# Group pipelines around the typed attention and the message pass of a four-layer graph network, with products made as rows and weights laid out ahead

## The chip, the cores and the metric

The kernel runs on one NeuronCore of one Trainium2 chip. The metric is the device time of one execution in microseconds (us). TensorE (PE) is clocked at one of two levels, 1.2 or 2.4 GHz; the profile gives the granted clock as a share of the full one. All arithmetic is in float32 unless bf16 is named.

## The reference

A graph of 3125 nodes with 128 features and 50000 edges, sorted by destination, goes through four residual layers. Each has the form `x = x + layer(relu(layernorm(x)))`.

```
x = x + gine(h)        3 rounds: relu(x[src] + ea64 @ We) summed per dst, two products, norm
x = x + rel_att(h)     for each of 5 edge types r: softmax over the edges of one dst of
                       leaky(Q_r[dst].a_q + K_r[src].a_k), sum of V_r[src] * attn; then elu
x = x + typed_att(h)   below
x = x + message(h)     below

typed_att:  Q, K, V = h @ block-diagonal W_Q, W_K, W_V of the node's type (3 types, 8 heads of 16)
            kt = K[src] @ W_edge[edge type]         (5 types)
            score = (Q[dst] * kt).sum(-1) / sqrt(16) * mu[head, edge type]
            w = softmax(score) over the edges of one dst; agg = sum of V[src] * w
            h1 = layernorm(h + agg @ W_out + b_out) * g1 + b1
            y  = layernorm(h1 + gelu(h1 @ W1 + b1) @ W2 + b2) * g2 + b2'
message:    m = relu([h[src], h[dst], ea32] @ W1.T + b1) @ W2.T + b2;  agg = sum of m per dst
            y = layernorm(h + relu(agg @ Wu.T + bu)) * gamma + beta
```

## The kernel before, in words

**Tiling.** The nodes are padded to 25 blocks of 128 rows (`NBLK`), and a node array is a tile of 128 x 3200. The edges lie in 416 tiles of 128 slots, so that no tile straddles a block; four tiles make one of 104 batches. "Groups" are 7 runs of up to four blocks (the last has one), 512 columns, one PSUM bank each. Products of whole arrays (`product`, L1709) run over 8 groups of 400 columns.

**Edge loops.** Each layer has one or two loops over the 104 batches. The five engines each have a program of their own; `run(engine, stages)` walks the batches and calls each stage with its lag, so that engines are several batches apart and wait for each other's semaphores. Every batch of a gathering loop takes four indirect DMAs of 128 rows on GpSimd (POOL): from `table_rel` (L714, first relation attention: value rows per node and edge type), `table_keys_values` (L723, typed attention: rows of 256 values, one per node and edge type), and `table_msg` (L696, message pass). Sums per destination are products with one-hot tiles, added to an array in SBUF or, where a sum stays in PSUM over a whole loop, opened and closed by seven products of one zero row (128x512, L1940, L2031, L2058).

**Order of the work around the change.** Between loops the program goes through stages that are separated by `Join` barriers: `join.to("x")` makes an engine wait until all engines have arrived there. In order:

- `rel_vectors`: PE makes for every block the value rows of the 5 edge types (L1866 128x512, L1867 128x128), ACT evacuates them (L1527, L1528), SP writes them to `table_rel`. Then come the score lookups over the batches (`lookups`, L1879, L1880, with DVE `pick_k`, L1100), while POOL gathers ahead and the values go to DRAM; then softmax sums per segment; then the loop `att_lookups`/`att_sums`. Its sums lie in seven PSUM banks.
- `rel_out`: ELU and the norm over the whole 128 x 3200 array on DVE (`norm`, L745 to L770; per-block statistics by L748, then 3200-column operations).
- `tr_clear` to `tr_values`: masks of the three node types multiply the array into three copies (L739), 75 transposes (L1698) with ACT copies of 512 columns (L1436), keys with the typed weights (L1709, 24 of 400 columns), Q and V (L2017, 75 of 256 columns) with ACT copies and bf16 splits of Q into three parts on DVE (`split`), then keys by edge type (L2024, L2025), which DVE multiplies by `mu` while it evacuates (L739, 125 of 128x128), and SP writes keys and values to `table_keys_values`.
- `trA` and `trB`: two loops over the batches, the first for scores and maxima with the gathers, the second for the weighted sums; `tr_zero` between them.
- `tr_mean` to `tr_out`: division by the softmax sum, 25 transposes, the product with W_out in transposed form, transposes back, sum and norm, 25 transposes, four hidden products with Gelu on ACT, the product with W2, transposes back, sum, norm, sum with X, norm. SP loads the weights of each part when the stage begins.
- `mp_weights` to `mp_table`: transposes, products of the two node parts of W1, one evacuated by DVE as node terms (L739 128x512), the other transposed back into the table and written in one DMA of 1600 KB.
- `mp`: per batch DVE makes a one-hot (float32, L739 128x512), PE transposes it (L1951) and ACT copies it (L1584); PE adds for each tile the edge product (L2103) and the lookup of node terms (L2104); DVE adds the gathered rows, ACT takes the ReLU, PE sums (L1734), DVE accumulates.
- `mp_sumT` to `mp_out`: transposes of the sums and of the degrees, product with W2 plus a one-row product for the bias (L1709, b2row), product with Wu, transposes back, norm, last sum and the output in two DMAs.

## Time and profile before

| what | value |
| --- | --- |
| three runs | 5188.26, 5188.58, 5203.77 us (median 5188.58) |
| profiled execution, its own time | 5186.52 us |
| its span in the trace | 5184.8 us |
| mean granted clock | 0.747 |
| busy: PE, DVE, POOL, ACT | 3185.8 (61%), 2685.6 (52%), 2938.1 (57%), 782.1 (15%) us |
| DMA | 561.85 MB, mean 108 GB/s |

No engine is busy for more than 61% of the span, so the shares alone name no bound: stages with different limits follow each other. A line of the profile's list of groups names the source line, the engine, the operation, what it writes and reads, the shape and the count; behind the first bar come busy time and the mean of one in ns, behind the second the idle time of the engine just before these instructions and what ended most of it. A float32 product has two records in such lists.

### The profile page before, as it was taken

What the parts mean: (1) busy time and instruction counts of PE and PEld (TensorE: products, weight loads), DVE (VectorE), ACT (ScalarE), POOL (GpSimd) and SP (SyncE); (2) the same over time, 40 slices, a digit from 0 to 9 for tenths busy, and PEclk for the clock granted to TensorE, in tenths of its full rate; (3) what the DMA queues carried; (4) which work ended last, traced back from release to release, by engine and by line L of the source; (5) the groups of instructions that cost most, each with busy time, mean ns of one, the idle gap of its engine ahead of it and who ended that gap; (6) DMA issues with size and microseconds to landing.
All of it is one profiled execution on the core that took longest, in us unless ns stands there. A gap on an engine that the chain in (4) does not pass through costs nothing. (4 is left out here: it accounts for less than half of the span.)

```text
span 5184.8 us, 84388 instructions
## 1 busy us (share of the span) xinstructions
PE 3185.8 (61%) x20680; PEld 2748.7 (53%) x20681; DVE 2685.6 (52%) x7818; ACT 782.1 (15%) x1810; POOL 2938.1 (57%) x2911
## 2 busy tenths in 40 slices
PE   0000298885777677775554676657776886566665
PEld 0000188885666566664552465445655884356663
DVE  5100288875444444445679655356664664344443
ACT  1000022222111111112100243100000001222222
POOL 3767677774777477771677740067773000077772
PEclk9999989886555555556655798855555997799997
DMA  6333355553222322222872573466654441022222
GB/s 214 75 87 77 93 153 151 150 140 76 76 76 77 60 77 75 76 76 62 214 202 88 172 193 100 109 170 174 175 171 106 123 127 47 4 72 62 62 61 32
DMA packets 631530, 561.85 MB, mean 108 GB/s; under 512 B 236605, under 2 KB 523650, under 8 KB 631426
## 3 DMA queue, kind: packets, MB, share of 16 engines
q0 software_dynamic: 99328, 211.51, 17.4%
q1 hardware_dynamic: 392322, 233.28, 15.5%
q10 hardware_dynamic: 139776, 115.91, 7.9%
q8 instruction: 38, 0.62, 0.0%
q14 instruction: 66, 0.54, 0.0%
HBM read 408.99 MB, written 151.40 MB: 108 GB/s over the span
## 5 line engine op out<-in xcount | busy, mean ns | idle before, releaser
L696 POOL DMA_INDIRECT ring<-table_gine,idx x1248 | 1244.2, 997 | 496.8 <-issue 370.3
L696 POOL DMA_INDIRECT ring<-table_msg,idx x416 | 425.0, 1022 | 725.4 <-SPq L191 598.9
L739 DVE TENSOR_TENSOR mraw<-ps,ring 128x512 f32<-128x512 f32 x416 | 287.4, 691 | 827.0 <-DMA ring<-table_gine,idx 372.4
L723 POOL DMA_INDIRECT arena<-table_keys_values,idx x416 | 429.7, 1033 | 466.1 <-SPq L191 337.8
L1777 PE MATMUL ps<-oh,msg 128*128 128x128 f32 x1664 | 425.5, 436 | 307.5 <-DVE HA L739 211.7
L714 POOL DMA_INDIRECT HA<-table_rel,idx x416 | 444.5, 1068 | 253.8 <-DMA table_rel<-arena 127.3
L739 DVE TENSOR_TENSOR HA<-HA,ps 128x128 f32 (+1 forms) x1664 | 476.5, 286 | 166.9 <-DVE HA L739 146.2
L1777 PEld LDWEIGHTS ps<-oh,msg 128*128 128x128 f32 x1664 | 366.4, 324 | 366.1 <-DVE HA L739 337.1
L1744 PE MATMUL ps<-wt,ear 65*128 65x128 f32 x2496 | 521.1, 379 | 16.7 <-DMA ear<-edge_attr_T 16.7
L682 POOL DMA_INDIRECT slot_records<-arena,slotr x400 | 390.3, 976 | 214.6 <-issue 122.2
L1744 PEld LDWEIGHTS ps<-wt,ear 65*128 65x128 f32 x2496 | 494.1, 293 | 17.4 <-issue 16.9
L739 DVE TENSOR_TENSOR oh<-iota_n,dl 128x512 f32<-128x512 f32 x624 | 431.0, 691 | 40.9 <-DVE small L739 28.5
L1466 ACT ACTIVATE msg<-mraw 128x512 f32<-128x512 f32 x416 | 262.0, 630 | 1254.5 <-DVE mraw L739 1189.4
L1754 PE MATMUL ps<-ident,small 128*128 128x128 f32 x416 | 70.2, 294 | 586.6 <-DVEq L915 586.2
L1754 PEld LDWEIGHTS ps<-ident,small 128*128 128x128 f32 x416 | 52.2, 160 | 589.2 <-issue 574.2
L1985 PE MATMUL ps<-gm,oh 128*128 128x9 f32 x832 | 194.9, 364 | 168.5 <-DVE small L739 168.1
L1734 PE MATMUL ps<-msg,oh 128*128 128x128 f32 (+1 forms) x1664 | 251.2, 298 | 68.5 <-DVE HA L739 66.8
L1985 PEld LDWEIGHTS ps<-gm,oh 128*128 128x128 f32 x832 | 185.2, 328 | 181.9 <-DVE small L739 154.5
L1734 PEld LDWEIGHTS ps<-msg,oh 128*128 128x128 f32 x1664 | 220.5, 206 | 92.4 <-DVE HA L739 57.8
L835 DVE TENSOR_SCALAR slotr<-arena 125x8 int32 (+1 forms) x50 | 9.9, 197 | 483.4 <-DMA arena<-in_edge_attr 479.1
L1914 PE MATMUL ps<-KP,iota_b 128*128 128x176 bf16 (+1 forms) x1602 | 215.8, 279 | 31.8 <-DVEq L1179 31.8
L2049 PE MATMUL ps<-msg,oh 128*128 128x128 f32 x832 | 195.3, 325 | 36.8 <-issue 32.9
(332 smaller groups left out, 6062.1 us busy)
## 6 DMA issues: line engine op xcount, KB each, us to landing
ear<-edge_attr_T SPq DMA_DIRECT2D x312, 128.0 KB
ear<-slot_rows ACTq DMA_DIRECT2D x312, 128.0 KB
oh<-slot_rows ACTq DMA_DIRECT2D x104, 256.0 KB
slot_values<-HA SPq DMA_DIRECT2D x104, 256.0 KB, 2.8
ring<-slot_values ACTq DMA_DIRECT2D x104, 256.0 KB
slot_values<-arena SPq DMA_DIRECT2D x104, 256.0 KB, 3.8
ring<-slot_values SPq DMA_DIRECT2D x104, 256.0 KB, 3.0
slot_records<-msg SPq DMA_DIRECT2D x32, 650.0 KB, 11.7
```

What stands on the lines that cost most here:

```text
L682: pool.indirect_dma_start(out=rec[:, :], out_offset=bass.IndirectOffsetOnAxis(ap=slotr[:, h, c:c + 1], axis=0), in_=recb[:, h, c, :], in_o ...
L696: pool.indirect_dma_start(out=ring[:, k % 4, j, 0:width], out_offset=None, in_=table[:, :], in_offset=bass.IndirectOffsetOnAxis(ap=idx[:, ...
L714: pool.indirect_dma_start(out=vdeep[:, k % DEEP, j, :], out_offset=None, in_=tab1[:, :], in_offset=bass.IndirectOffsetOnAxis(ap=idx5[:, k ...
L723: pool.indirect_dma_start(out=kvring[:, k % 4, j, :], out_offset=None, in_=tab2[:, :], in_offset=bass.IndirectOffsetOnAxis(ap=idx5[:, k * ...
L739: return V.tensor_tensor(o, x, y, op)
L1466: A.activation(msg[:, t.s4, :, 0:D], mraw[:, t.h], ACT.Relu).then_inc(q["relu"], 1)
L1734: ins = M.matmul(out_of(t, j), oh[:, t.s4, j, :], x, start=True, stop=True)
L1744: ins = M.matmul(ps[:, t.s4 if t.of else t.h, j * P:(j + 1) * P], ear[0:EA + 1, t.h, j * P:(j + 1) * P], wt[0:EA + 1, o:o + D], start=True ...
L1777: ins = M.matmul(ps[:, 4 + t.s4, j * P:(j + 1) * P], msg[:, t.s4, j, 0:D], oh[:, t.s4, j, :], start=True, stop=True)
L1914: M.matmul(ps[:, 6, 512 - w:512], iota_b[:, :], KP[:, :, :].rearrange("p i c -> p (i c)")[:, 0:w], start=False, stop=False)
L1985: ins = M.matmul(ps[:, 6 + t.h, 9 * j:9 * j + 9], oh[:, t.s4, j, :], gm[:, t.s4, j, 0:9], start=True, stop=True)
L2049: M.matmul(psf[:, bass.ds(blocks[j] * D, D)], oh[:, t.s4, j, :], msg[:, t.s4, j, 0:D], start=False, stop=False)
```

## The change

No arithmetic on the whole is added or dropped except where named. Its parts:

- **A, value rows of the relation attention.** The 25 pairs of value products and their ACT copies are a stage of the lookup loop, one block per turn, ahead of that turn's lookups (`run(..., head=HEADK)` writes out the first 28 turns).
- **B, into the typed attention.** The zero products that open and close PSUM sums are bf16. ELU runs by groups: ACT makes relu(-x) and exp from PSUM, DVE adds; the norm is centred and scaled per block, 18 of 25 blocks scaled on ACT. Edge weights, mu, two bias rows and the node types (one row broadcast to 128 partitions, 1.6 MB) are loaded beside the loop before; mu and 1/sqrt(16) are multiplied into the edge weights. Only one array is transposed; three DVE operations per group compare the type row and multiply, reading PSUM. PE goes through the groups as in the first listing below; ACT evacuates 512 columns of the typed keys per block, DVE 128. The five joins between are gone. At the end DVE adds b_out to H and ln2_b to X.
- **C, beside the first typed loop.** SP loads 21 weight tensors of the later stages ahead of its per-batch work.
- **D, from the typed attention to the message pass.** Everything runs by groups without joins. The products with W_out and W2 are made as rows (data as the stationary side), so that the transposes back are gone. The message pass's W2 and Wu are folded into one 128x128 matrix here. Norms are per block as in B. The message table is written in seven DMAs, one a group, and node terms are split in three bf16 parts (`NP`).
- **E, the message loop.** ACT's queue fetches the slots' row numbers, broadcast to 128 partitions (128 KB a batch); DVE makes the transposed one-hot from them in bf16; the PE transposes and the ACT copy are gone; the lookup is three bf16 products a tile. The stages' lags grow by one.
- **F, after the message loop.** One pipeline by groups: transpose, one product of the folded weight, one product of 33 rows that adds degree times b2 and the bias (`DG`, `KR`); ReLU and sum as rows, norm per block with ACT scales, last sum by groups, output in four DMAs.

```diff
+HEADK = -(-(NBLK + 1) // 4)
 tensor, relation attention
-            for b in range(NBLK):
...
-                M.matmul(ps[:, s, :], hb, wt[:, RELW:RELW + 512], start=True, stop=True)
-                M.matmul(ps[:, s + 1, 0:D], hb, wt[:, RELW + 512:RELW + NREL * D], start=True, stop=True).then_inc(vt_ps, 1)
             pe.wait_ge(dve_made, kq_set)
-            run(pe, [(2, lookups)])
+            run(pe, [(2, lookups), (0, value_products)], head=HEADK)
             for z in range(7):
-                M.matmul(ps[:, z, 0:n], b2row[0:1, :], any_row[:, 0:n], start=True, stop=False)
+                M.matmul(ps[:, z, :], zero_b, any_b, start=True, stop=False)
 vector, into the typed attention
-            ch(V.tensor_scalar(neg, relsum, 0.0, None, ALU.min))
...
-            norm(X[:, :, :], H[:, :, :], relu=True)
-            join.to("rel_out")
+            for z in range(GRP + 1):
...
+                    V.scalar_tensor_tensor(Xf[:, at], T[0][:, at], -1.0, Xf[:, at], ALU.add, ALU.add).then_inc(cent, 1)
+                if z:
...
+                        V.bn_stats(lnst[:, b, :], X[:, b, :]).then_inc(bn_done, 1)
+            feature_sums()
+            for b in range(NBLK):
+                V.tensor_scalar(H[:, b, :], X[:, b, :], stat[:, 0, b:b + 1], 0.0, ALU.subtract, ALU.max).then_inc(cent, 1)
...
+                    for t in range(NTYPE):
+                        V.scalar_tensor_tensor(MXT[:, i % 2, t, 0:n], TROW[:, at], float(t), ps[:, i % 2, 0:n], ALU.is_equal, ALU.mult).then_inc(cent, 1)
...
+                    V.tensor_copy(kwb[:, z % 2, 0:nz, 4 * D:], ps[:, 7, 0:nz * D].rearrange("p (j d) -> p j d", j=nz)).then_inc(cent, 1)
+            ch(tt(H[:, :, :], H[:, :, :], per_feature(bout_row), ALU.add))
+            ch(tt(X[:, :, :], X[:, :, :], per_feature(ln2b_row), ALU.add))
 vector, message loop
+            def mp_dst_onehots(t):
...
+                V.tensor_scalar(oN[:, t.h], nrow[:, t.h], iota_p, None, ALU.is_equal).then_inc(qp["onehotT"], 1)
-            run(dve, [(4, acc_pair(qp, agg3, D + 1)), (2, mp_add), (0, onehots(qp["onehot"], qp["sums"], oh))])
+            run(dve, [(5, acc_pair(qp, agg3, D + 1)), (3, mp_add), (1, mp_dst_onehots), (1, onehots(qp["onehot"], qp["sums"], oh))])
 scalar, message loop
-            run(act, [(2, relu(qp)), (0, onehotT(qp, lambda t: t.n))])
+            def mp_rows_in(t):
...
+                act.dma_start(nrow[:, t.h], slotrow[1:2, bass.ds(t.k * B, B), :].rearrange("w t s -> w (t s)")
+                              .to_broadcast([P, B * P])).then_inc(drin[t.s4], 16)
+            run(act, [(0, mp_rows_in), (4, relu(qp))])
 tensor, message loop
-                    M.matmul(o, ear[:, t.h, j * P:(j + 1) * P], wt[:, 0:D], start=True, stop=False)
-                    ins = M.matmul(o, ohT[:, t.h, j, :], rows_at(T3[2], D)(blocks[j]), start=False, stop=True)
+                    M.matmul(o, ear[:, t.h, j * P:(j + 1) * P], MW[:, 0:D], start=True, stop=False)
+                    for i in range(3):
+                        ins = M.matmul(o, oN[:, t.h, j * P:(j + 1) * P], rows_at(NP[i], D)(blocks[j]), start=False, stop=(i == 2))
-            run(pe, [(3, sums(qp, D + 1, pair(D + 1))), (1, nd_mp), (0, turn_onehot(qp, own))])
+            run(pe, [(4, sums(qp, D + 1, pair(D + 1))), (2, nd_mp)])
 gpsimd
-            join.to("mp_table")
+            join.to("tr_zero")
+            pool.wait_ge(t_out, 16 * (7 + NBLK + GRP))
             gathers(qp, "added", tab3, D, idx1)
 tensor, after the message loop
+            M.transpose(ps[0:NBLK, 7, 0:P], agg3[:, :, D], ident[:, :]).then_inc(pn_full, 1)
+            for i in range(GRP + 1):
...
+                        M.matmul(o, DG, KR[:, b * D:(b + 1) * D], start=True, stop=False)
+                        ins = M.matmul(o, T[1][:, b * P:(b + 1) * P], W_c, start=False, stop=True)
```

How the instructions move, at three places. **PE between the closing of the relation sums and the typed keys.** A row is the line, the operation, what it writes and reads, the shape and how many in a row; HA is H, the array that the norm writes, arena holds the transposed arrays, wt the Q, K and V weights, score the edge weights. Before:

```order
L1940 MATMUL ps<-X,b2row 128x512 x7
L1698 MATMUL ps<-ident,arena 128x128 x50
L1698 MATMUL ps<-ident,HA 128x128 x25
L1709 MATMUL ps<-arena,wt 128x400 x24
L2017 MATMUL ps<-wt,arena 128x256 x75
L2024 MATMUL ps<-score,arena 128x512
L2025 MATMUL ps<-score,arena 128x128
```

Of the change:

```order
L2156 MATMUL ps<-TY,b2row 128x512 x7
L2229 MATMUL ps<-ident,HA 128x128 x8
L2238 MATMUL ps<-arena,wt 128x512 x3
L2245 MATMUL ps<-wt,arena 128x256 x12
L2229 MATMUL ps<-ident,HA 128x128 x4
L2238 MATMUL ps<-arena,wt 128x512 x3
L2245 MATMUL ps<-wt,arena 128x256 x12
L2254 MATMUL ps<-score,arena 128x512 x4
L2258 MATMUL ps<-score,arena 128x128 x4
```

The 75 transposes became 25, and each group of four blocks goes through all four kinds of product, with the typed keys two groups behind the transposes.

**PE between the closing of the typed sums and the second norm's input.** L1709 is any product of 400 columns, L1698 any transposition. Before:

```order
L2058 MATMUL ps<-wt,b2row 128x512 x7
L1698 MATMUL ps<-ident,arena 128x128 x25
L1709 MATMUL ps<-arena,wt 128x400 x8
L1698 MATMUL ps<-ident,arena 128x128 x50
L1709 MATMUL ps<-arena,wt 128x400 x35
```

Of the change, from the folding of the weights on (L2305 to L2308):

```order
L2305 MATMUL ps<-ident,arena 128x128
L2307 MATMUL ps<-arena,msg 128x128
L2308 MATMUL ps<-arena,small 25x128
L2315 MATMUL ps<-ident,arena 128x128 x8
L2324 MATMUL ps<-arena,wt 128x512 x4
L2315 MATMUL ps<-ident,arena 128x128 x4
L2324 MATMUL ps<-arena,wt 128x512 x4
L2333 MATMUL ps<-wt,oh 128x128 x16
```

The hidden products (L2324) and the products with W2 as rows (L2333, 16 a group) follow each other group by group, and no transposition back stands behind them.

**PE in one batch of the message loop.** ear is the edge features, ohT the transposed one-hot, and the TENSOR_LOAD and ISA rows take the block numbers. Before:

```order
L1951 MATMUL ps<-ident,oh 128x128 x4
L1734 MATMUL ps<-msg,oh 128x129 x4
L293 TENSOR_LOAD nb
L2103 MATMUL ps<-wt,ear 128x128
L2104 ISA
L2104 MATMUL ps<-arena,ohT 128x128
```

Of the change (the tile's rows; three of its four tiles follow in the same way):

```order
L2364 MATMUL ps<-arena,ear 128x128
L2366 ISA
L2366 MATMUL ps<-arena,ohT 128x128
L2366 ISA
L2366 MATMUL ps<-arena,ohT 128x128
L2366 ISA
L2366 MATMUL ps<-arena,ohT 128x128
```

The four transpositions at the batch's head are gone, and each tile has three lookups in the place of one.

## Rows read from the trace of the kernel before

**Rows 1.** One line's instructions, relation attention: ns min/median/max, first and last start.
```profile
L1866 PE MATMUL ps<-wt,arena x50: 592/595/1201, 2430.7 to 2469.3; 128*128 128x512 f32 x50
...
L1879 PE MATMUL ps<-KP,ohT x1248: 215/310/313, 2477.2 to 2710.0; 128*128 128x125 bf16 x179
...
L714 POOL DMA_INDIRECT HA<-table_rel,idx x416: 940/944/7363, 2478.4 to 3048.5; - x139
```

**Rows 2.** Stretches: length; PE, PEld, DVE, ACT, POOL busy; PEclk; DMA; GB/s.
```profile
2430.00:2477.00 47.00, 33.74 (x104) 18.05 (x104) 2.78 (x9) 19.14 (x50) 0.00 (x0) 0.90 0.51 188
2477.00:2711.00 234.00, 147.03 (x1664) 133.78 (x1664) 166.22 (x932) 23.29 (x105) 177.09 (x183) 0.58 0.84 215
3202.00:3262.00 60.00, 10.49 (x17) 3.75 (x15) 39.24 (x51) 4.38 (x3) 0.00 (x0) 0.52 0.04 1
3295.00:3331.00 36.00, 32.57 (x151) 28.35 (x151) 13.20 (x20) 11.13 (x50) 0.00 (x0) 1.00 0.83 228
3331.00:3387.00 56.00, 35.35 (x100) 17.93 (x100) 26.96 (x125) 0.00 (x0) 0.00 (x0) 0.90 0.53 147
3387.00:3944.00 557.00, 380.92 (x2190) 316.30 (x2190) 345.93 (x1161) 19.40 (x98) 428.75 (x415) 0.50 0.62 172
4331.00:4401.00 70.00, 25.61 (x86) 13.37 (x84) 30.41 (x48) 13.47 (x24) 0.00 (x0) 0.62 0.04 10
4401.00:4458.00 57.00, 53.23 (x154) 26.46 (x154) 0.00 (x0) 28.65 (x48) 0.00 (x0) 0.95 0.01 3
4458.00:4544.00 86.00, 20.30 (x150) 17.84 (x150) 49.54 (x86) 12.81 (x24) 0.00 (x0) 0.64 0.09 25
4544.00:5094.00 550.00, 377.81 (x2872) 336.71 (x2873) 243.80 (x606) 125.57 (x205) 423.62 (x415) 0.98 0.25 62
5110.00:5147.00 37.00, 33.36 (x123) 16.24 (x123) 0.00 (x0) 18.91 (x36) 0.00 (x0) 0.92 0.00 1
5147.00:5185.00 38.00, 0.11 (x1) 0.00 (x0) 27.54 (x39) 0.65 (x3) 0.00 (x0) 0.54 0.14 42
```

**Rows 3.** The page's list of groups: the gathers of three loops on POOL.
```profile
L696 POOL DMA_INDIRECT ring<-table_msg,idx x416 | 425.0, 1022 | 725.4 <-SPq L191 598.9
...
L723 POOL DMA_INDIRECT arena<-table_keys_values,idx x416 | 429.7, 1033 | 466.1 <-SPq L191 337.8
...
L714 POOL DMA_INDIRECT HA<-table_rel,idx x416 | 444.5, 1068 | 253.8 <-DMA table_rel<-arena 127.3
```

**Rows 4.** One line's instructions: the products that close and open the sums in PSUM.
```profile
L1940 PE MATMUL ps<-X,b2row x14: 587/1056/1056, 3202.4 to 3211.4; 1*128 1x512 f32 x14
...
L2031 PE MATMUL ps<-wt,b2row x14: 1056/1056/1214, 3982.0 to 3993.3; 1*128 1x512 f32 x14
```

**Rows 5.** Groups of instructions, shapes apart, from 3210 to 3387 us.
```profile
L2017 PE MATMUL ps<-wt,arena 128*128 128x256 f32 x150 | 32.6, 380 | 0.6 <-ACTq L191 0.6
...
L739 DVE TENSOR_TENSOR arena<-ps,small 128x128 f32<-128x128 f32 x125 | 27.0, 283 | 25.8 <-DMA table_keys_values<-arena 14.1 <-PE ps L2024 10.2 <-PE ps L2025 1.4
L1709 PE MATMUL ps<-arena,wt 128*128 128x400 f32 x48 | 16.4, 501 | 0.4 <-POOLq L191 0.4
...
L739 DVE TENSOR_TENSOR X<-X,arena 128x3200 f32<-128x3200 f32 x2 | 7.0, 3492 | 0.1
```

**Rows 6.** Groups of instructions, shapes apart, from 4331 to 4544 us.
```profile
L1436 ACT ACTIVATE arena<-ps,col 128x400 f32<-128x400 f32 x40 | 23.6, 593 | 25.4 <-PE ps L1709 24.4
...
L1436 ACT ACTIVATE arena<-ps 128x512 f32<-128x512 f32 x36 | 20.9, 597 | 75.9 <-PE ps L1698 68.4 <-PE ps L2084 7.2
...
L748 DVE BATCH_NORM_STATS2 lnst<-arena 128x6 f32<-128x128 f32 x50 | 9.9, 276 | 0.1
L2058 PE MATMUL ps<-wt,b2row 1*128 1x512 f32 x14 | 9.2, 820 | 0.0
```

**Rows 7.** One line's instructions: scaling of one block on ACT in an earlier layer.
```profile
L1519 ACT ACTIVATE HA<-HA,stat x18: 384/386/402, 2409.8 to 2414.7; 128x128 f32<-128x128 f32 x18
```

**Rows 8.** Groups of instructions, shapes apart, from 3387 to 3944 us.
```profile
L1261 DVE TENSOR_SCALAR ohT<-ear,pcol 128x512 bf16<-128x512 bf16 x102 | 34.3, 336 | 8.1 <-DMA ear<-slot_rows 6.0 <-PE ps L1975 1.9
```

More of the change, by code:

```diff
@@ L1379, in _ @@
+            ch(V.tensor_scalar(rden, psf[:, NPAD:NPAD + NBLK * NHEAD], 1e-10, None, ALU.add))
             ch(V.reciprocal(rden, rden))
[L1380 to L1387 removed]
@@ L1521, in _, with value_rows @@
             join.to("rel_vectors")
-            for b in range(NBLK):
+            def value_rows(t):
+                b = t.k
+                if not isinstance(b, int) or b >= NBLK:
+                    return
                 if b >= 2:
@@ L1679, in _ @@
+            for z in range(GRP):
+                at, n = turned_group(z)
+                act.wait_ge(pn_full, tfull["at", z])
+                A.activation(T[1][:, at], ps[:, z % 2, 0:n], ACT.Copy).then_inc(pn_free, 1)
+            scale(T3[0], tmade["c4"], NBLK)
         @block.tensor
```

773 lines of the change are left out of this document (501 added, 272 removed).

## The prediction

> **What bounds the kernel now.** I read the stretches first, because the shares of the whole span name no engine. In a row of [rows 2] the five busy times are those of PE, PE's weight loads, DVE, ACT and POOL. Two kinds of stretch differ. The loops (here 2477 to 2711, 3387 to 3944 and 4544 to 5094) are long and have one engine at work nearly all the time. In the message loop that is POOL: its 415 gathers are busy for 423.6 of 550 us, and the rest is a gap of 0.30 us behind each. From [rows 3], (425.0 + 725.4 - 598.9)/416 = 1.326 us for each gather, 5.30 a batch, while PE is busy for only 377.8 and DVE for 243.8 us. The second kind is the stages between the loops: 3202 to 3387 (185 us), 4331 to 4544 (213 us) and 5110 to the end at 5184.8 (75 us), where POOL has nothing and the others take turns. From 3202 to 3262 PE has 10.5 busy us of 60 and DVE 39.2; from 4331 to 4544 PE has 25.6 + 53.2 + 20.3 = 99 of 213; in the last 38 us PE has 0.1. These 473 us are a chain of barriers, and most of the change is there.
>
> **Prices.** PE's dense rate in float32 at full clock: 75 products of 256 columns in 32.6 us, 24 of 400 in 16.4 us [rows 5], both 1.70 ns a column; at half clock 512 columns take 1056 ns a pass where 587 is the shortest [rows 4], so up to twice that. ACT takes 0.60 us for 512 columns [rows 6]; it scales a block in 4.9/17 = 0.29 us [rows 7]. DVE takes 3.49 us for a 3200-column operation [rows 5], 0.20 for one block's statistics (9.9/50) [rows 6]. I estimate DVE's centring of a block at 0.2 to 0.26, from that row and 128/3200 of 3.49 = 0.14 plus a fixed part, and the small statistics operations with the square root and its table load at 3.5 to 4 us.
>
> **A, value rows.** Before, 25 blocks run from 2430.7 to 2469.3 [rows 1] and the lookups start at 2477.2, 2.24 us a batch (232.8/104). Now they share turns. A turn costs PE 147.0/104 = 1.41 for the lookups and 33.7/25 = 1.35 for the value products [rows 2], about 2.9 with handovers. From about 2433 (the DVE work that precedes the lookups is 2.8 us) the 23rd lookup is done at 2433 + 25 x 2.9 = 2506; before it was done at 2477.2 + 23 x 2.24 = 2529. That is 23 us; I take **-20**. At half clock a turn takes 3.5 us: -8. If DVE's 2.24 set the pace: -39. Range -5 to -35. POOL's gathers still start only when the table is whole, now some 30 us later; before they ran from 2478.4 to 3048.5 [rows 1], 150 us ahead of the end of the loop that uses the last of them (3202), so they bind nothing.
>
> **B, into the typed attention, 185 us before.** Closing in bf16: 1.7 instead of 10.1 (3202.4 to 3211.4 + 1.1, [rows 4]). ELU by groups: 14 ACT operations of 0.6 with a table load, last sum and statistics: 13. Statistics and root 3. Centring and scaling up to the first group's transposition 6, masks of the first group (three 512-column operations of 0.7) and handover 5. Then PE's stream: transposes 3200 columns, keys 9600, Q and V 19200, typed keys 16000, together 48000 x 1.70 = 81.6; half clock at its start +3; waits at the eighteen handovers +7. End: last typed keys to `kwb`, two DVE operations of 3.49, write landing: 8. Sum 128 against 185: **-58**, range -35 to -70. The 50 transposes less, 125 small DVE operations that PE waited on, and the type masks are what goes. On DVE the group work is 21 masks x 0.7 + 7 splits of about 2.2 + 7 copies, some 35 us beside PE's 82: covered.
>
> **Opening of the second typed loop.** 3982.0 to 3993.3 + 1.1 = 12.3 us [rows 4], now seven bf16 products of 512 columns. Lookups in bf16 of up to 125 columns take 147.0/1664 = 0.09 at clock 0.58 [rows 2], so 512 columns 0.36 to 0.43: 3 us. **-8** (-4 to -12).
>
> **C, SP's 21 loads** stand ahead of the score write-backs of the first typed loop. An issue costs SP under half a us by estimate, so 10 us once, against a loop of 557 us; POOL runs ahead by four batches (21 us). **0** (0 to +6).
>
> **D, 213 us before.** Closing 1.7 instead of 9.2 [rows 6], reciprocal 1.8, mean, transposes and W_out rows in one pipeline of 6400 columns 13, last sum and statistics 2; statistics and root 4; centring, scales and bias to the first group 9; PE: transposes 3200, hidden 12800, W2 rows 12800 columns, 28800 x 1.70 = 49, half clock at the start 3, last handover 3; last sum 2; root 4; 25 scales on ACT with the centring beside 9; last X sum 2; root 3.5; centring and scaling 6; node pipeline, seven groups of which DVE takes about 3 us each (sum 0.7, split in three parts), 17; last table write 3.5. Sum 133: **-80**, range -60 to -92. What went: eleven barriers, weights loaded in the stage's own time, 75 transposes back at 1.70 x 128 ns, a dozen 3200-column DVE operations. ACT stays hidden in the feed-forward part: 28 Gelus of about 0.7 + 7 x 0.6 = 24 us beside PE's 49.
>
> **E, the message loop.** PE loses four transposes and four float32 lookups a batch and gets twelve bf16 ones; ACT loses 0.60 a batch; DVE gets a bf16 one-hot of 0.34 [rows 8] and has 2.3 of 5.3 us used. None of this was the bound, so the price is what the new DVE operation does to POOL. Nearest rows: the first typed loop has such a one-hot in each batch [rows 8], and its gathers take (429.7 + 466.1 - 337.8)/416 = 1.341, +0.015 x 416 = +6; the relation loop with twice as wide ones has (444.5 + 253.8 - 127.3)/416 = 1.373, +19. I take **+5**, range 0 to +20. That PE's work falls is worth nothing while POOL is the bound.
>
> **F, after the message loop, 75 us before.** 9600 columns at 1.70 = 16.3 with half clock at the start 20; last sum and statistics 2; root 3; 25 ACT scales 7.3; last sum 1; last output 3.5. Sum 37: **-38**, range -30 to -42.
>
> **Sum.** -20 - 58 - 8 + 0 - 80 + 5 - 38 = -199. Against the profiled execution's own 5186.5 (span 5184.8): 4987.5. The median of the runs is 2 above it: **4990**.
>
> **The rivals.**
>
> 1. *PE at half clock in the new pipelines.* After loops and chains at low PE load PE comes in at 0.5: the whole first typed loop has 0.50 with PE busy 381 of 557 us [rows 2]. For it: 3202 to 3262 and 4331 to 4401 stand at 0.52 and 0.62. Against it: as soon as PE worked densely it was granted 0.9 to 1.0 (3295 to 3387, 4401 to 4458, 5110 to 5147). Interleaved groups with waits are less dense. If all of it ran at half: B +80, D +46, F +16, so 5130; half of that, 5060. Chance 0.10.
>
> 2. *The gathers are held up by the one-hots.* If each bf16 one-hot held POOL for its full 0.34 us, the loop would be 104 x 0.34 = 35 us longer, not 5: 5020. For it: gathers are slowest in the loops that have such operations [rows 3]. Against: the first typed loop has one a batch and its gathers cost 0.06 us a batch more, not 0.34. Chance 0.12. The Trainium skill, "SBUF — State Buffer", section "Who interferes with whom", says that a DVE tensor_scalar in a 2-port mode holds the port pair shared with GpSimd for its whole length, and that the other fully blocks; by that rule the sum would be 5020. The trace does not agree in the size: its own loop with this operation shows a sixth of it.
>
> 3. *The front is bound by the writes of the key table.* 25 blocks of two writes of 320 KB are 16 MB. Before they moved at 228 GB/s (share 0.83) for the values and 147 for the keys [rows 2]. At 147 they need 109 us instead of PE's 82: +25, 5015. Against: at 228 they need 70, and now both kinds go out evenly. Chance 0.08.
>
> 4. *Slower than before: the message loop leaves POOL as its bound.* Place: the chain row numbers, one-hot, lookup with two buffers. It decides when a batch takes over 5.30 us, and it would need 5.30 + 199/104 = 7.2 us to eat the whole gain. PE's price: 377.8/104 = 3.6 now, about half of it gone with 8 of 16 float32 products, 1.9 left; at half clock 3.8 and 12 x 0.09 = 1.1, so 4.9 at the worst. That reaches neither. Chance 0.02, at 5200.
>
> **How the numbers follow.** Forecast 0.68, with its own range 4955 to 5025 (terms off in both directions); rivals 0.10, 0.12, 0.08, 0.02. The range 4950 to 5045 takes in the second and third rival and leaves out the clock one and the slower one. A measurement of this kernel can tell about 0.3% (16 us) from no change. Only rival 4 or several misses together get back there: faster 0.97, same 0.01, slower 0.02.
>
> **What would show it.** In the profile after: from the closing products to the first gather of the typed loop about 127 us at a clock near 1; from the second typed loop's end to the first message gather about 133; the message loop's gathers at 1.33 to 1.35 us each and still the bound; 37 us behind the loop; lookups ending 20 us earlier. It is wrong if a pipeline's PE clock stays at 0.5, if PE waits on DVE in the node pipeline for over 3 us a group, or if the message loop shows POOL waiting for anything but its own issue.

## The result, and the profile after

The changed kernel takes 4977.18 us (median of four runs, 4968.22 to 4983.67) where the kernel before takes 5194.78 (four runs, 5188.26 to 5203.77): a ratio of 0.9579, 95% interval 0.9555 to 0.9603. The forecast was 4990 with a range of 4950 to 5045. The total is right; two of its terms, for the message loop (E) and for what follows it (F), are not, and they nearly cancel.

The profiled execution took 4978.06 us, its span is 4976.0 (before 5186.52 and 5184.8). Its stretches, in the order of columns of [rows 2]:

```profile
2442.00:2514.00 72.00, 53.67 (x465) 36.71 (x466) 36.31 (x201) 19.99 (x67) 0.00 (x0) 0.94 0.64 183
2514.00:2697.00 183.00, 115.86 (x1295) 105.35 (x1294) 127.20 (x726) 19.35 (x86) 131.42 (x134) 0.58 0.81 213
3190.00:3220.00 30.00, 8.48 (x24) 4.01 (x23) 24.13 (x85) 13.38 (x34) 0.00 (x0) 0.58 0.00 0
3220.00:3298.00 78.00, 77.67 (x305) 51.55 (x303) 25.65 (x49) 27.14 (x58) 0.00 (x0) 0.99 0.69 190
3298.00:3306.00 8.00, 0.00 (x0) 0.00 (x0) 7.62 (x5) 0.00 (x0) 0.12 (x1) 0.66 0.74 205
4246.00:4270.00 24.00, 14.20 (x93) 11.94 (x90) 18.71 (x59) 7.07 (x16) 0.00 (x0) 0.79 0.00 1
4270.00:4325.00 55.00, 50.80 (x281) 36.63 (x281) 28.43 (x68) 28.63 (x52) 0.00 (x0) 0.91 0.00 1
4325.00:4347.00 22.00, 0.00 (x0) 0.00 (x0) 20.89 (x86) 8.78 (x31) 0.00 (x0) 0.57 0.00 0
4347.00:4373.00 26.00, 17.76 (x125) 16.22 (x125) 20.77 (x51) 11.94 (x30) 0.00 (x0) 0.83 0.27 79
4373.00:4897.00 524.00, 377.52 (x2874) 346.50 (x2875) 276.09 (x719) 64.25 (x102) 397.38 (x415) 0.82 0.37 90
4913.00:4955.00 42.00, 41.72 (x126) 29.76 (x126) 8.01 (x27) 4.13 (x8) 0.00 (x0) 0.50 0.00 1
4955.00:4976.00 21.00, 0.19 (x1) 0.00 (x0) 13.62 (x48) 7.63 (x26) 0.00 (x0) 0.50 0.25 76
```

The front of the typed attention (3190 to 3306) is now nearly one block of PE work: 77.7 busy us of 78 at a clock of 0.99. Behind the message loop (4913 to 4955) PE is just as full, 41.7 of 42, but at 0.50. The page's groups for the gathers, against [rows 3]:

```profile
L811 POOL DMA_INDIRECT ring<-table_msg,idx x416 | 398.3, 958 | 630.3 <-DMA table_msg<-arena 503.7
...
L838 POOL DMA_INDIRECT arena<-table_keys_values,idx x416 | 435.2, 1046 | 335.8 <-DVEq L186 207.3
...
L829 POOL DMA_INDIRECT HA<-table_rel,idx x416 | 447.1, 1075 | 292.0 <-DMA table_rel<-arena 165.4
```

The message gathers fell from 1022 to 958 ns, which no term of the forecast had: with the gap behind it one takes (398.3 + 630.3 - 503.7)/416 = 1.262 us, where 1.326 was measured before and 1.33 to 1.35 forecast. The lines of the relation attention, the closing and the opening, against [rows 1, 4]:

```profile
L2100 PE MATMUL ps<-wt,arena x50: 592/676/1222, 2442.7 to 2514.2; 128*128 128x512 f32 x50
...
L2088 PE MATMUL ps<-KP,ohT x1248: 215/268/313, 2447.1 to 2697.2; 128*128 128x125 bf16 x179
...
L2156 PE MATMUL ps<-TY,b2row x7: 374/374/385, 3190.5 to 3191.8; 1*128 1x512 bf16 x7
...
L2264 PE MATMUL ps<-TY,b2row x7: 601/629/629, 3906.2 to 3908.7; 1*128 1x512 bf16 x7
```

With the first and last starts of these lines in both traces, the span falls into pieces that sum to the whole difference:

| piece | before | after | difference | forecast |
| --- | --- | --- | --- | --- |
| start to the first layer's last gather (not changed) | 2350.2 | 2358.6 | +8.4 | 0 |
| A: from there to the last lookup | 359.8 | 338.7 | -21.1 | -20 |
| last lookup to closing of the relation sums | 492.4 | 493.3 | +0.9 | 0 |
| B: closing to the first typed gather | 184.8 | 115.3 | -69.5 | -58 |
| first typed gather to the opening (C is here) | 594.8 | 600.3 | +5.5 | 0 |
| opening to closing of the typed sums | 349.3 | 340.2 | -9.1 | -8 |
| D: closing to the first message gather | 212.9 | 127.0 | -85.9 | -80 |
| E: first to last message gather | 550.5 | 523.9 | -26.6 | +5 |
| F: last message gather to the end | 90.1 | 78.8 | -11.3 | -38 |
| sum | 5184.8 | 4976.1 | -208.7 | -199 |

How far one execution stands for a kernel shows where the same kernel ran again (e5, below): 2352.2, 339.6, 502.3, 113.8, 595.7, 344.2, 126.1, 522.9 and 79.2 us for the nine pieces. B, D, E and F repeat within 2 us; the long loops move by 4 to 9, so that the +8.4 and the +5.5 are no effect of the change.

### The profile page after: what moved, and what is told of

Its sections match the earlier page's. It is cut to its first block, busy times and chain, and to the rows that moved or that the text cites. A ratio compares the mean times of both kernels' runs of the same rounds, so it can differ in the third digit from the quotient of the medians.

```text
span 4976.0 us, 85301 instructions
## 1 busy us (share of the span) xinstructions
PE 3122.3 (63%) x20716; PEld 2741.5 (55%) x20717; DVE 2700.0 (54%) x8043; ACT 721.8 (15%) x1742; POOL 2927.5 (59%) x2911
## 3 DMA queue, kind: packets, MB, share of 16 engines
q1 hardware_dynamic: 389624, 235.01, 16.3%
## 4 chain that ended last, share of the span: by engine, by line
POOL 50%; issue 20%; PE 14%; DMA 8%; DVE 5%; ACT 1%; SPq 1%; DVEq 0%; POOLq 0%; ACTq 0%
POOL ring L811 29%; POOL HA L829 8%; POOL arena L838 8%; POOL slot_records L797 5%; PE ps L2282 3%; PE ps L2131 2%; DMA ring<-table_gine,idx 2%; DMA arena<-in_edge_attr 2%; DMA table_rel<-arena 1%; PE ps L2283 1%; PE ps L2149 1%; PE ps L2245 1%; DMA slot_records<-arena,slotr 1%; PE ps L1950 1%; DVE HA L854 1%
## 5 line engine op out<-in xcount | busy, mean ns | idle before, releaser
L811 POOL DMA_INDIRECT ring<-table_gine,idx x1248 | 1249.6, 1001 | 498.3 <-issue 370.2
L811 POOL DMA_INDIRECT ring<-table_msg,idx x416 | 398.3, 958 | 630.3 <-DMA table_msg<-arena 503.7
L854 DVE TENSOR_TENSOR mraw<-ps,ring 128x512 f32<-128x512 f32 x416 | 287.7, 691 | 779.4 <-DMA ring<-table_gine,idx 344.1
L1960 PEld LDWEIGHTS ps<-wt,ear 65*128 65x128 f32 x2496 | 491.5, 292 | 16.9 <-issue 16.3
L854 DVE TENSOR_TENSOR oh<-iota_n,dl 128x512 f32<-128x512 f32 x624 | 432.1, 693 | 31.5 <-DVE small L854 25.9
L1950 PE MATMUL ps<-msg,oh 128*128 128x128 f32 (+1 forms) x1664 | 283.6, 323 | 213.2 <-DVE HA L854 210.2
L1950 PEld LDWEIGHTS ps<-msg,oh 128*128 128x128 f32 x1664 | 240.5, 222 | 252.0 <-DVE HA L854 208.3
L2364 PE MATMUL ps<-arena,ear 128*128 128x128 f32 x832 | 221.1, 355 | 10.7 <-DVE ohT L1595 10.7
```

Source lines behind the costliest of these rows:

```text
L811: pool.indirect_dma_start(out=ring[:, k % 4, j, 0:width], out_offset=None, in_=table[:, :], in_offset=bass.IndirectOffsetOnAxis(ap=idx[:, ...
L854: return V.tensor_tensor(o, x, y, op)
L1950: ins = M.matmul(out_of(t, j), oh[:, t.s4, j, :], x, start=True, stop=True)
L1960: ins = M.matmul(ps[:, t.s4 if t.of else t.h, j * P:(j + 1) * P], ear[0:EA + 1, t.h, j * P:(j + 1) * P], wt[0:EA + 1, o:o + D], start=True ...
L2364: M.matmul(o, ear[:, t.h, j * P:(j + 1) * P], MW[:, 0:D], start=True, stop=False)
```

## The experiments

Two questions are open: why the gathers became shorter (E), and why the end gained so little (F). The runs fall into two kinds by the chip that they used. On one, the kernel before takes 5181 to 5195 us and POOL's gap behind a message gather is 0.305 us, as in the traces above; on the other it takes 6243 to 6307 us and the mean gap is 0.55 to 0.6, since gathers land later and POOL waits for buffers: DVE's addition starts 1.8 us behind the end of its batch's last message gather in the trace of after, 17.6 us behind it in e3. The first kind has e5 to e8 and e12, the second e1 to e4 and e9 to e11; each comparison stays on one kind, called the short-gap and the long-gap chip. The kernel before has a trace on the short-gap chip alone.

**E, theory T1: a gather waits where it starts.** In the trace of before (columns: start us, us, engine, line, operation, count, idle before), an ordinary gather and a long one:

```profile
4700.08 0.94 POOL L696 DMA_INDIRECT ring<-table_msg,idx  x1 [0.30 <-issue]
...
4701.04 0.68 DVE L739 TENSOR_TENSOR oh<-iota_n,dl 128x512 f32<-128x512 f32 x1
4701.32 1.22 POOL L696 DMA_INDIRECT ring<-table_msg,idx  x1 [0.30 <-issue]
```

The float32 one-hot (DVE, both inputs in SBUF) ran from 4701.04 to 4701.72; the gather that started at 4701.32 took 1.22 us and not 0.94. In the trace of after, the same operation starts behind the gather's start, and the gather takes 0.94:

```profile
4639.97 0.34 DVE L1595 TENSOR_SCALAR ohT<-ohT,pcol 128x512 bf16<-128x512 bf16 x1
...
4641.58 0.94 POOL L811 DMA_INDIRECT ring<-table_msg,idx  x1 [0.30 <-issue]
4641.76 0.68 DVE L854 TENSOR_TENSOR oh<-iota_n,dl 128x512 f32<-128x512 f32 x1
```

I paired all one-hots with every gather that they overlap. Before, 97 began 0 to 0.4 us ahead of a gather, and 94 of these gathers were over 0.05 us longer, by 0.23, 0.30 and 0.42 us in the mean for a head start of 0.35, 0.25 and 0.15: always the time from the gather's start to the one-hot's end, less 0.13. (In the other three the one-hot had begun less than 0.04 us ahead.) Together the loop's gathers are 32.5 us longer than 416 of 0.944. Of the 25 gathers during which a one-hot began, one was stretched. After, 9 one-hots began 0 to 0.4 us ahead and 4 gathers were stretched.

That it is an operation with both inputs in SBUF, and not any work of DVE, the first layer of the same trace shows: 65 of its gathers started while DVE ran an addition that takes one input from PSUM (`arena<-ps,small`, `mraw<-ps,ring`) with 0.2 us or more of it left, and none was over 0.003 us longer; 68 started under a float32 one-hot, and 64 of them were stretched. In program order the bf16 one-hot (0.34 us) now stands between the addition that waits for a batch's gathers and the float32 one-hot. By the traces it pushes that one just past the next gather's start; no run took it out alone.

Theory T1 is that this position against the gathers makes their length. Its rival R1 is that the change's shorter PE and ACT work, or the bf16 one-hot itself, made them shorter. Edit of e1 and e6 (on the kernel before) and of e2 and e7 (on the change), in the message loop alone (in the change the stage has the lag 1):

```diff
-                    for _ in range(3):
+                    for _ in range(after):     # 3 everywhere, 2 in the message loop
...
-(0, onehots(qp["onehot"], qp["sums"], oh))
+(0, onehots(qp["onehot"], qp["sums"], oh, after=2))
```

Expected of e1:

> The kernel before; in the message loop alone DVE's float32 one-hot is issued after the third of the four accumulations, not after the fourth (0.45 us earlier in the batch). In the trace of before 95 gathers of this loop are stretched by 0.35 us, all where that one-hot was already running when the gather started (it began 0.1 to 0.5 us ahead of it). Theory T1 (phase: a gather that starts while a DVE operation with two SBUF inputs runs waits for its end): the one-hot now ends at about the gather's start; mean gather of table_msg falls from 1022 to 945 to 975 ns, first to last gather from 550.5 to 520 to 535 us, the whole by 15 to 30 us. Rival R1 (the change's shorter PE and ACT work, or its bf16 one-hot, is what made its gathers shorter): no change here, 1022 ns and 550 us within 5.

Expected of e2:

> The changed kernel with the same one number: the float32 one-hot of the message loop after the third accumulation. In its trace this one-hot starts 0.0 to 0.4 us behind a gather's start, and 0.45 us earlier it would be running when the gather starts. T1: about one gather a batch is stretched by 0.2 to 0.4 us; mean gather rises from 958 ns to 1010 to 1040, first to last gather from 523.9 to 545 to 560 us, the whole by 20 to 35 us. R1: no change, 958 ns and 524 us within 5.

Both ran on the long-gap chip. The page's group of e1, of e2, and of e3, which has the change's message loop untouched:

```profile
L696 POOL DMA_INDIRECT ring<-table_msg,idx x416 | 401.6, 965 | 853.7 <-SPq L191 602.9
```

```profile
L811 POOL DMA_INDIRECT ring<-table_msg,idx x416 | 425.2, 1022 | 729.7 <-DMA table_msg<-arena 500.3
```

```profile
L811 POOL DMA_INDIRECT ring<-table_msg,idx x416 | 399.8, 961 | 764.0 <-DMA table_msg<-arena 509.7
```

The length of a gather follows the edit (961 to 1022 ns between e3 and e2), the time does not: first to last gather 653.7 us in e2, 653.2 in e3. e1 took 0.9998 of the kernel before (0.9979 to 1.0018), where T1 had expected 15 to 30 us less, and e2's 20 to 35 us did not come either. With the long gap POOL is not the bound, and a longer gather only shortens its wait. The same edits were then measured on the short-gap chip, with the change itself beside them. Expected of the change, e5:

> The changed kernel as it is, as the neighbour of the next three on the same chip. On the chip of the first four runs gathers landed later and POOL waited 0.55 to 0.6 us behind each (0.305 in the traces of before and of the change), so that shorter gathers could not show in the time there. If POOL's gap is 0.305 on this chip: gathers of table_msg 958 ns, first to last 524 us, last gather to end 79 us, total near 4977.

Expected of e6:

> The kernel before with its message loop's float32 one-hot issued after the third accumulation, as in the first run. T1, if POOL's gap is 0.305: gathers 945 to 975 ns instead of 1022, first to last gather 520 to 535 us instead of 550, and 15 to 30 us less than the kernel before. R1: 1022 ns, 550 us and no difference.

Expected of e7:

> The changed kernel with the float32 one-hot after the third accumulation, as in the second run. T1, if POOL's gap is 0.305: gathers about 1022 ns (as in the second run) instead of 958, first to last gather 547 to 555 us instead of 524, about 25 us more than the change itself. R1: no difference.

The groups of e6 and of e7, and the place in e7 where a gather is long again:

```profile
L696 POOL DMA_INDIRECT ring<-table_msg,idx x416 | 395.0, 950 | 728.4 <-SPq L191 601.9
```

```profile
L811 POOL DMA_INDIRECT ring<-table_msg,idx x416 | 416.2, 1000 | 631.0 <-DMA table_msg<-arena 504.6
```

```profile
4639.58 0.95 POOL L811 DMA_INDIRECT ring<-table_msg,idx  x1 [0.30 <-issue]
...
4640.51 0.69 DVE L854 TENSOR_TENSOR oh<-iota_n,dl 128x512 f32<-128x512 f32 x1
4640.83 1.19 POOL L811 DMA_INDIRECT ring<-table_msg,idx  x1 [0.30 <-issue]
```

| short-gap chip | gather | first to last | total |
| --- | --- | --- | --- |
| before | 1022 ns | 550.5 us | 5193.5 |
| e6: before, one-hot a step earlier | 950 | 520.6 | 5149.05, ratio 0.9918 (0.9888 to 0.9948) |
| e5: the change | 955 | 522.9 | 4975.1, ratio 0.9579 (0.9539 to 0.9619) |
| e7: the change, one-hot a step earlier | 1000 | 541.7 | 4991.16, ratio 0.9595 (0.9567 to 0.9623) |

T1 holds in both directions: the old kernel gains 30 us in its message loop from one number, and the change loses 19 of its 27. The gathers that are over 0.05 us longer fall from 94 to 15 in e6 and rise from 9 in each of the two traces of the change (after, e5) to 100 in e7. R1 falls, since PE, ACT and the bf16 one-hot are the same within each pair. e7's gathers are 1000 ns and not the 1022 expected; the one-hot there begins 0.4 to 0.5 us ahead in 40 of 98 cases, so that less of it is left when the gather starts. Of e6's 44 us between the medians, 30 are in this loop; the rest lies in parts that were not edited.

**F, theory T2: the 33-row product.** In the trace of after, the two products that alternate behind the loop:

```profile
L2388 PEld LDWEIGHTS ps<-score,gm x50: 285/308/334, 4915.3 to 4953.8; 33*128 33x128 f32 x50
L2388 PE MATMUL ps<-score,gm x50: 417/498/579, 4915.3 to 4954.1; 33*128 33x128 f32 x50
...
  issue: 5.9, 24
```

The weight loads pause 24 times, 5.9 us in all, for nothing that the profile shows; in the order of time, 0.72 us lie between one product's start and the next's. Theory T2 is that the alternation of 33 and 128 rows makes these pauses and holds the clock down; its rival R2 is that the loop ahead sets the clock. Edit of e3 (`0:65` in e10):

```diff
-        KR = score[0:33, 0:NPAD]
+        KR = score[:, 0:NPAD]
-        DG = gm[:, :, :, :].rearrange("p a b c -> p (a b c)")[0:33, 0:P]
+        DG = gm[:, :, :, :].rearrange("p a b c -> p (a b c)")[:, 0:P]
```

> The changed kernel; behind the message loop the product that adds degree times b2 and the bias contracts over 128 rows, 95 of them zero, and not over 33. In the trace of the change PE is busy without a break from 4920 to 4950 there and its clock stays at 0.50, and a product takes 0.72 us where a dense float32 one of 128 columns takes 0.43 at half clock; last gather to end 78.7 us. Theory T2 (the change of the row count makes PE drain between products, 0.29 us each, and keeps it from its clock): products 0.43 us or less, the clock rises to 1 within 10 us, last gather to end 52 to 60 us. Half of T2 (drain only): clock stays 0.50, last gather to end 62 to 68 us. Rival R2 (the clock is held by the loop before, the row count costs nothing): 78 us within 2.

Measured on the long-gap chip: last gather to end 55.1 us in e3, 84.8 and 77.7 in e2 and e4, which have the 33 rows. The line and two stretches of e3, the second with the products:

```profile
L2388 PEld LDWEIGHTS ps<-score,gm x50: 190/192/333, 6069.6 to 6083.5; 128*128 128x128 f32 x50
L2388 PE MATMUL ps<-score,gm x50: 275/275/582, 6069.6 to 6083.6; 128*128 128x128 f32 x50
```

```profile
6064.00:6070.00 6.00, 3.01 (x19) 2.48 (x20) 2.62 (x9) 1.24 (x3) 0.00 (x0) 0.91 0.00 0
6070.00:6080.00 10.00, 10.00 (x82) 10.00 (x82) 4.02 (x12) 2.01 (x4) 0.00 (x0) 0.89 0.01 2
```

T2 holds in full: the pauses are gone, the clock is 0.9, and the end is 23 to 30 us shorter. Two consecutive products start 0.22 us apart in e3 and 0.72 in the change. At half clock without pauses it would be 0.43, so of the 26 us between the two streams of PE work (41.6 and 15.9 us) about 50 x 0.29 = 14.5 are by estimate the pauses, and the rest is the clock. Could the clock have come from the loop ahead instead? e4 put PE's old work back into the loop:

```diff
+            def fill(t):
+                for j in range(B):
+                    M.transpose(ps[:, t.h, j * P:(j + 1) * P], ident[:, :], ident[:, :])
-            run(pe, [(4, sums(qp, D + 1, pair(D + 1))), (2, nd_mp)])
+            run(pe, [(4, sums(qp, D + 1, pair(D + 1))), (2, nd_mp), (0, fill)])
```

> The changed kernel; PE makes four float32 transpositions of the identity a batch in the message loop, which nobody reads, in the place of those that the change took out. R2 (the clock behind the loop depends on how busy PE is in the loop): mean clock of the loop 0.95 to 1 instead of 0.82, the clock behind it 0.9, last gather to end 58 to 66 us. T2 alone: the loop's clock rises, the end stays at 0.50 and 78 us. The gathers stay at 950 to 965 ns in either case; if the traffic of PE mattered to them (R1), they would rise towards 1020.

Three stretches of e4: the loop, its drain, the products:

```profile
5406.00:6066.00 660.00, 461.93 (x3232) 413.50 (x3233) 268.22 (x707) 63.22 (x101) 398.77 (x415) 0.78 0.30 71
6066.00:6081.00 15.00, 10.19 (x96) 9.39 (x96) 9.56 (x30) 2.35 (x4) 1.46 (x2) 0.99 0.36 25
6090.00:6110.00 20.00, 20.00 (x62) 14.29 (x61) 3.78 (x12) 1.79 (x3) 0.00 (x0) 0.50 0.00 0
```

The drain stands at 0.99, and with the alternating products the clock falls to 0.50 all the same; the end takes 77.7 us. R2 falls. (Its own forecast for the loop, 0.95 to 1, was missed too: 0.78 on this chip, where batches are longer.) The gathers stayed at 962 ns (e3: 961), though PE had more to do: one more point against R1. How many rows decide it? e10:

> The changed kernel with the bias product on 65 rows, 32 of them zero, in the place of 33. If what costs is the change between products of 33 and of 128 rows as such, any count under 128 does it: products 0.72 us, clock 0.50, last gather to end 79 us. If it is that 33 rows take a part of the array and 65 take all of it (the edge products of the first layer have 65 rows, and their weight loads wait 16.9 us in all for 2496): as with 128 rows, last gather to end 54 to 56 us, clock 0.9 or more.

```profile
L2388 PEld LDWEIGHTS ps<-score,gm x50: 190/191/338, 6025.7 to 6040.5; 65*128 65x128 f32 x50
L2388 PE MATMUL ps<-score,gm x50: 272/275/579, 6025.7 to 6040.6; 65*128 65x128 f32 x50
```

Last gather to end 56.3 us: 65 rows behave as 128 do, but for a clock of 0.85 over the products where 0.9 or more was expected. So it isn't the change of the row count as such; somewhere between 33 and 65 rows lies a limit. The Trainium skill, "TensorEngine Tiling (Array Packing)", section "Key Properties", says that changing the tiling mode drains TensorE, and the page lists row tilings of 64 and 32 rows. If a product of 33 rows runs in such a mode, which no trace shows, e3 and e10 agree with it, with 0.72 us a product at half clock on 33 rows and 0.22 on 65 and 128. What that does to the granted clock it does not say; over these products it was 0.50 in all six traces with 33 rows (after, e2, e4, e5, e7, e9) and 0.85 to 0.96 in the five with 65 or 128 (e3, e8, e10, e11, e12).

**A alone.** e9 puts the 25 value products and evacuations back ahead of the lookups:

```diff
+            for b in range(NBLK):
+                value_products_of(b)
             pe.wait_ge(dve_made, kq_set)
...
-            run(pe, [(2, lookups), (0, value_products)], head=HEADK)
+            run(pe, [(2, lookups)])
...
+            for b in range(NBLK):
+                value_rows(Batch(b // 4, b % 4))
...
-            run(act, [(0, lookup_rows_in), (1, value_rows), (3, q_copied)], head=HEADK)
+            run(act, [(0, lookup_rows_in), (3, q_copied)])
```

> The changed kernel with part A undone: all 25 value products and their evacuations ahead of the lookups, as before. Theory TA (the lookups are what is waited for, part A gives what it takes off their end): from the first layer's last gather to the last lookup 360 us instead of 339, and the whole 15 to 20 us longer. Rival RA (the loop that follows takes it back: the table's gathers start some 40 us later in the change and run further into that loop, whose length was 337 us in one trace of the change and 346 in two, 337 in both of before): lookups end 20 us later, the loop is 5 to 10 us shorter, the whole 8 to 15 us longer.

It was measured on the long-gap chip, where the lookups take 760 us and not 230. From the first layer's last gather to the last lookup it took 882.2 us (e10 and e11: 871.3, 870.9), the stretch up to the closing 475.8 (478.7, 478.8). Part A is worth 11 us there and 3 are given back. The totals do not show it: e9's, 6102.3 us (6087 to 6140), lies 21 over e10's (two runs, 6065 and 6097), and 24 of that are F's, so that neither TA's 15 to 20 us nor RA's 8 to 15 can be read there. On the short-gap chip only pairs of whole kernels bear on it: 359.8 and 356.5 us without A (before, e6), 338.7 and 339.5 with it (after, e5). And RA has something: the stretch behind took 492.4 and 492.9 without A, but 493.3, 502.4, 501.6, 503.8 and 499.5 with it (after, e5, e7, e8, e12). Both stretches together take 852 and 849 us without A and 832 to 845 with it. So A nets -5 to -20, -11 between the means; whether the giving back comes from the later gathers or from the type rows loaded in that loop was not tried.

**A version that beats both.** e8 joins the two findings, the rows as in e3 and the one-hot of the first layer:

```diff
-                one = onehots(qg["onehot"], qg["sums"], oh)
+                one = onehots(qg["onehot"], qg["sums"], oh, after=3 if l == 0 else 1)
```

> The changed kernel with two edits: the bias product behind the message loop on 128 rows (as in the third run), and in the second and third round of the first layer the float32 one-hot after the second accumulation instead of the fourth (0.9 us earlier, where by T1 it ends ahead of a gather's start; 48 of 110 one-hots there stretch a gather by 0.44 us in the trace of the change). If POOL's gap is 0.305: mean gather of those rounds 950 to 965 ns instead of 997 to 999, 13 to 20 us less in each; last gather to end 55 us instead of 79; 50 to 60 us less than the change in all, near 4920. If T1 fails for that layer: only the 24 us at the end. On a chip with the long gap: only the 24 us too.

It takes 4911.97 us, a ratio of 0.9447 (0.9421 to 0.9473) to before, against 0.9579 for the change. Its groups:

```profile
L811 POOL DMA_INDIRECT ring<-table_gine,idx x1248 | 1205.5, 966 | 498.1 <-issue 368.8
L811 POOL DMA_INDIRECT ring<-table_msg,idx x416 | 396.8, 954 | 647.9 <-DMA table_msg<-arena 521.4
```

The mean over the first layer's three rounds is 966 ns (after 1001); the second and third round have 950 and 945, where 950 to 965 was expected. The first layer's last gather starts at 2313.1 us instead of 2352.1 in e5, and last gather to end takes 53.8 instead of 79.2. Both gains, 39 and 25 us, are there; in the profiled execution 13 are lost in the second typed loop (357.5 us from opening to closing, e5 344.1), whose clock stayed low for 80 us. That execution was the slowest of the four (4928.57 us), and the medians lie 63 us apart, so the loss need not be that of every run. Three stretches of 20 us from its opening on:

```profile
3866.00:3886.00 20.00, 16.61 (x90) 13.88 (x91) 7.61 (x21) 2.20 (x5) 0.00 (x0) 0.50 0.48 136
3926.00:3946.00 20.00, 20.00 (x125) 20.00 (x123) 8.07 (x20) 0.92 (x4) 0.00 (x0) 0.50 0.30 88
3946.00:3966.00 20.00, 17.87 (x188) 17.31 (x186) 13.02 (x33) 1.60 (x7) 0.00 (x0) 0.99 0.41 111
```

e11 and e12 add a third edit, in the first typed loop, and take `after=1` in the first round of the first layer too:

```diff
+            def max_dst_onehots_later(t):
+                for _ in range(3):
+                    yield
+                max_dst_onehots(t)
-(6, end_onehots), (1, max_dst_onehots)])
+(6, end_onehots), (1, max_dst_onehots_later)])
```

> The changed kernel with the bias product on 128 rows, the float32 one-hot after the second accumulation in all three rounds of the first layer, and, in the first loop of the typed attention, the bf16 one-hot issued four steps later, so that it does not follow the float32 one-hot at once. T1 refined: a gather is held at its start only, until the DVE operations that have the port then have ended, and a chain of two (0.69 + 0.38 us) holds it for up to 1 us. In that loop and in the first layer's first round the one-hots are spread evenly against the gathers, so only the chain's length counts: with L the length and 1.25 us between gathers, L*L/2.5 a batch, 0.46 for the chain, 0.25 for the two apart, 22 us in 104 batches. Expected: gathers of the typed loop 0.97 to 1.00 us instead of 1.036, its first to last gather 540 to 550 us instead of 558 to 563; the first round unchanged (1.003 to 1.010 us) since its phases are spread; second and third round 0.945 to 0.955; the whole 4885 to 4905. If the chain is not what holds them: that loop unchanged, the whole 4912.

On the long-gap chip the typed loop's gathers took 974 ns (e9, e10: 1026, 1018), and its time stayed: 728.1 us to the opening (e10 728.3). Expected of the same kernel again, e12:

> The three edits again, in case this chip has POOL's short gap of 0.305 us (the chip of the last call had 0.55 to 0.7, and only the gathers' own length could be read there: 0.974 us in the typed loop instead of 1.018 to 1.026, as T1 refined said). If so: typed loop's first to last gather 540 to 548 us instead of 555 to 563, the first round of the first layer unchanged, the whole 4885 to 4905 and 8 to 20 us under the eighth run's 4912. If the chip has the long gap again: no difference from the last call.

```profile
L838 POOL DMA_INDIRECT arena<-table_keys_values,idx x416 | 414.5, 996 | 352.0 <-DVEq L186 217.4
...
L811 POOL DMA_INDIRECT ring<-table_gine,idx x1248 | 1204.9, 965 | 495.5 <-issue 366.3
```

On the short-gap chip: 4901.27 us, a ratio of 0.9456 (0.9427 to 0.9485). The typed loop's first to last gather is 548.2 us (e8 555.1, e5 558.7), gathers 996 ns instead of 1036: inside the lengths expected, while the stretch is at the edge of its range, since some of it went into waits (POOL's mean gap rose from 0.309 to 0.324 us). The first round stayed at 1001 ns (e5 1005), as expected: its one-hots begin at all places against the gathers, and moving them all by a step changes nothing. Against e8 the ratio shows no difference.

## Why the prediction was right, and where it was not

- **What bounds the kernel.** Right: 155 of the 209 us come out of the two barrier chains (B, D), which the stretches of [rows 2] named.
- **A.** Right for the lookups: the 25 value products start 2.95 us apart (2442.7 to 2514), where 2.9 was said for a turn. That nothing behind it takes back was too plain: 1 to 11 us are on the short-gap chip.
- **B, -58 forecast, -69 measured.** The terms stood on the high side (and add up to 128.3, which makes -57). From closing to the first transposition 19.7 us (23.7 said), from there to the last typed key 87 (96.6 said for masks, stream, half clock and waits: the masks of the next group ran beside the products, and only 3.5 us of waits for DVE are left), then 8.4 (8 said). The dense rate of 1.70 ns a column was right for the products; a transposition took half of it, 0.11 us for 128 columns (L2229), so that its 3200 columns were priced 2.7 us too high here, and again in D and in F. Rival 3 (key writes as the bound) did not come: 3220 to 3298 moved 190 GB/s with PE never waiting.
- **D, -80 and -86.** To the first transposition of the feed-forward 24 us (31.5 said), feed-forward 53 (55), to the node pipeline 24 (26.5), node pipeline to the first gather 26 (20.5): DVE takes 3.0 us a group there, as said, but 4.6 us pass between the first transposition (4347.4) and the first product (4352.0), which the sum had left out.
- **C and the opening.** Opening to closing -9.1 for -8 (-5 between before and e5); the opening itself went from 12.3 us to 3.1, where 3 was said. The 5.5 us in the first typed loop are not C's: e5 took 595.8 us with C, e6 595.9 without.
- **E, +5 forecast, -27 measured: the step "the price is what the new DVE operation does to POOL".** I priced the new operation by loops that have one, and took its sign from them. What counted was not which operations a loop has, but which one is running when a gather starts. The rows behind the bound mixed both: the typed loop's gathers are long in part because float32 and bf16 one-hots follow each other there without a pause (apart, 996 ns instead of 1036 in e12, 974 instead of 1018 in e11; 0.944 is an undisturbed one). Rival 2 fell. The Trainium skill, "SBUF — State Buffer", section "Who interferes with whom", says that issue order decides who blocks, and the traces agree: what counts is whether the one-hot or the gather starts first. But of a tensor_tensor with two SBUF inputs it infers that descriptor generation is not held, and here 94 gathers were. Which port or read of the gather waits, no run shows. And the bf16 one-hot, the operation that rival 2 feared, started inside a gather 74 times in the message loop of the change, and these gathers were longer by at most 0.014 us in the mean. Like the float32 one it holds a gather only where it already runs as the gather starts: 6 gathers with a head start of 0.1 to 0.2 us were longer by 0.05 us in the mean, 11 in e8 by 0.07, and not by its 0.34.
- **F, -38 forecast, -11 measured: the term "9600 columns at 1.70 = 16.3 with half clock at the start 20".** The stream took 41.6 us (4913.3 to 4954.9). I priced every product at the dense rate of products over 128 rows, though 25 of them have 33. On 65 or 128 rows last gather to end is 54 to 56 us, 16 to 18 of them the loop's drain: what is left is 37 to 39 us for the 37 forecast, though with a stream of 16 to 17 us where 20 was said and 22 behind it where 17 was. Rival 1 (half clock) named the symptom, but not for this cause, and in B and D it did not come.
- The two errors, -32 and +27, nearly cancel; B (-11) and D (-6) were better than said, and the loops that were not meant to change took 15 us back. That the total was inside the range is in part luck.

## What to carry to other kernels

Where a loop is bound by gathers issued from POOL, look at what DVE has running at the moment a gather starts, and move operations with two SBUF inputs by a step: one number was worth 30 us in a loop of 550, 0.6% of the old kernel. Where a float32 product over a few rows alternates with products over 128 (33 here; 34 to 64 were not tried), pad the short one with zero rows to 65 or more. And when a forecast's total is right, split it by stage before believing its terms.

## What the runs showed of the hardware that was not expected

- A gather that starts while DVE runs a float32 tensor_tensor with two SBUF inputs is longer by the time to that operation's end less 0.13 us (94 of 97 in before, within 0.02 us); one that is already under way when the operation starts is not touched (24 of 25). With one of the inputs in PSUM it is not touched either (65 gathers of the first layer, at most 0.003 us).
- Alternating float32 products over 33 and 128 rows: 0.72 us each, with the clock at 0.50 for 40 us of full PE, though in e4 it stood at 0.99 just ahead; over 65 or 128 rows 0.22 us each, at 0.85 to 0.96.
- After the opening of the second typed loop the clock came back at different times: some 30 us behind it in the trace of after (3936 to 3946 stands at 0.86), but only 80 us behind the opening, at about 3946, in e8, with PE busy 20 of 20 us meanwhile. The loop takes 334 to 358 us over all traces of the change. What decides the moment is open.
- Two kinds of chip, some 5190 and 6300 us for the same kernel: the lookups of the relation attention take 233 and 760 us (before and e1), the stages between the loops the same (B: 115.3 in after and 113.9 in e2, D: 127.0 and 127.8). Whether that is the chip or its state at the time, the runs cannot tell.
